# Folding the carried state into the first column of u*B on ScalarE, for ten of sixteen states

## The reference, cut to what matters

```
dt = softplus(einsum(dt_raw, W_dt) + b_dt)
A  = -exp(A_log)
dA  = exp(dt[..., None] * A)
dBx = dt[..., None] * Bm[:, :, None, :] * x[..., None]
def step(h, inp):
    dA_t, dBx_t, C_t = inp
    h = dA_t * h + dBx_t
    y = einsum('bds,bs->bd', h, C_t)
    return (h, y)
x = layernorm(x + scan + Dp * x)
x = layernorm(x + ffn(x))
```

## Time and profile before

| | |
|---|---|
| median of 3 runs | 2003.35 us (2001.41 to 2003.37) |
| profiled execution: time, span | 1997.66 us, 1995.8 us |
| PE busy | 1763.8 us (88%) |
| DVE busy | 1823.0 us (91%) |
| ACT busy | 1568.9 us (79%) |
| POOL busy | 1701.3 us (85%) |

### The profile page before, as it was taken

The page is one execution under the profiler, slowest core; times in us unless marked ns, Lnnn a source line. Parts: engine busy times, 40 slices in busy tenths (PEclk is TensorE's granted clock), DMA queues, the critical chain, the costliest instruction groups (busy, mean ns, idle before and its releaser), DMA issues.

```text
span 1995.8 us, 37091 instructions
## 1 busy us (share of the span) xinstructions
PE 1763.8 (88%) x11048; PEld 1384.4 (69%) x11048; DVE 1823.0 (91%) x2285; ACT 1568.9 (79%) x2924; POOL 1701.3 (85%) x779
## 2 busy tenths in 40 slices
PE   5788888988989988889888989889889898899986
PEld 4667677776777776777666777667767667776764
DVE  4899999999999999999999999999999999999994
ACT  6878878788887788778788787888777887887862
POOL 5998888898888988888888888988889888889880
PEclk7999999999999999999999999999999999999999
DMA  7323333333233233234233233232333332342300
GB/s 243 101 97 120 105 114 117 102 110 117 90 122 124 93 116 116 91 118 133 80 121 117 96 117 126 87 122 97 116 118 98 114 116 87 118 133 70 122 12 22
DMA packets 116565, 215.35 MB, mean 108 GB/s; under 512 B 11153, under 2 KB 45554, under 8 KB 116466
## 3 DMA queue, kind: packets, MB, share of 16 engines
q1 hardware_dynamic: 116466, 214.40, 32.8%
HBM read 195.48 MB, written 18.87 MB: 107 GB/s over the span
## 4 chain that ended last, share of the span: by engine, by line
PE 56%; issue 17%; DVE 16%; ACT 6%; POOL 3%; DVEq 1%; ACTq 0%; DMA 0%; POOLq 0%; SPq 0%
PE p_o L1001 17%; PE p_y L964 12%; DVE h L703 8%; PE p_m L988 6%; PE p_da L932 6%; PE p_c L941 3%; PE p_m L904 3%; DVE hid L747 3%; PE p_m L912 3%; PE p_y L957 2%; PE p_m L978 2%; DVE silu_g L741 2%; ACT da_k L537 2%; ACT p_da L537 1%; POOL ub L410 1%
## 5 line engine op out<-in xcount | busy, mean ns | idle before, releaser
L420 POOL TENSOR_TENSOR h<-h,c_bc 128x1024 f32<-128x1024 f32 x352 | 833.0, 2371 | 148.0 <-ACT h_carry L523 120.7
L410 POOL TENSOR_TENSOR ub<-u,b_bc 128x1024 f32<-128x1024 f32 x320 | 757.7, 2374 | 0.1
L964 PE MATMUL p_y<-ident,h 128*128 128x128 f32 x4096 | 533.3, 277 | 7.7 <-POOL h L420 4.4
L537 ACT ACTIVATE p_da<-dt,neg_a 128x512 f32<-128x512 f32 x640 | 432.1, 682 | 85.3 <-DVE h L703 81.8
L964 PEld LDWEIGHTS p_y<-ident,h 128*128 128x128 f32 x4096 | 476.2, 143 | 28.1 <-POOL h L420 13.6
L703 DVE TENSOR_TENSOR_SCAN h<-p_da,ub 128x512 f32<-128x512 f32 x320 | 381.1, 1213 | 29.8 <-ACT p_da L537 23.6
L703 DVE TENSOR_TENSOR_SCAN h<-p_da,h_carry,ub 128x512 f32<-128x512 f32 x320 | 399.9, 1271 | 1.4 <-ACT p_da L537 0.8
L551 ACT ACTIVATE ub_t<-u_t,bc_t 128x256 f32<-128x256 f32 x768 | 344.9, 497 | 28.9 <-issue 28.1
L1001 PE MATMUL p_o<-wt_down,hid 128*128 128x256 f32 x1536 | 354.8, 382 | 11.8 <-DVE hid L747 8.6
L932 PE MATMUL p_da<-ident,ub_t 128*128 128x128 f32 x1536 | 244.1, 296 | 126.5 <-DVE h L703 125.5
L1001 PEld LDWEIGHTS p_o<-wt_down,hid 128*128 128x128 f32 x1536 | 284.9, 190 | 67.3 <-issue 29.6
(11 more groups left out here) (101 smaller groups left out, 1813.4 us busy)
## 6 DMA issues: line engine op xcount, KB each, us to landing
c_bc<-bc_rows_dram SPq DMA_DIRECT2D x352, 256.0 KB, 5.1
b_bc<-bc_rows_dram SPq DMA_DIRECT2D x128, 512.0 KB, 5.3
x_in<-in_L_attn_x SPq DMA_DIRECT2D x32, 512.0 KB, 3.5
b_bc<-bc_rows_dram SPq DMA_DIRECT2D x64, 256.0 KB, 3.1
out_x<-res_n SPq DMA_DIRECT2D x32, 512.0 KB, 3.3
bc_rows_dram<-bc_rows SPq DMA_DIRECT2D x32, 64.0 KB, 1.6
hid<-in_L_ffn_w_gate SPq DMA_DIRECT2D x1, 768.0 KB, 4.9
hid<-in_L_ffn_w_up SPq DMA_DIRECT2D x1, 768.0 KB, 6.7
```

The source lines that it names most:

```text
L410: nc.gpsimd.tensor_tensor(ub[:, i % UB_SLOTS, :, :], u[:, par, :, :], b_bc[:, i:i + 1, :].broadcast_to([P, DH, T]), ALU.mult).then_inc(s_u ...
L420: nc.gpsimd.tensor_tensor(h[:, s % H_SLOTS, :, :], h[:, s % H_SLOTS, :, :], c_bc[:, i:i + 1, :].broadcast_to([P, DH, T]), ALU.mult).then_i ...
L537: nc.scalar.activation(da, dt[:, par, q, :], ACT.Exp, scale=neg_a[:, q, s:s + 1]).then_inc(s_da, 1)
L964: ins = nc.tensor.matmul(p_y_tok[:, k, q * P:(q + 1) * P], h[:, s % H_SLOTS, q, k * P:(k + 1) * P], ident[:, :], start=False, stop=(s == S ...
```

## The change

In par 1, for the ten B_STATES, DVE's scan no longer takes its initial value from `h_carry`: it takes the constant 0.0. To make that right, ACT first adds decay(first step) times carried state to the first column of u*B in `ub`, for each state and each q (`first_column`, 20 instructions of 128x1 in a par 1 chunk, in place), one state ahead and directly ahead of the decay of the same state and q. The decays of the first step for all states are made in par 0 by two instructions of 128x16 (`first_decay`, at state 8, zone 0). The scans of par 1 wait for the new semaphore s_first, for each q, and no longer for s_ub and s_carry. The six K_STATES stay as they are.

```
+    "first_decay": (8, 0), ...
+FIRST_AHEAD = 1
...
+            def first_decay(c, par, batch):
+                act.wait_ge(s_dt, c + 1)
+                for q in range(DH):
+                    nc.scalar.activation(da_first[:, q, :], neg_a[:, q, :], ACT.Exp,
+                                         scale=dt[:, par, q, 0:1]).then_inc(s_da_first, 1)
+
+            def first_column(c, s, batch, q):
+                i = B_STATES.index(s)
+                if q == 0:
+                    act.wait_ge(s_ub, NB * c + (i + 1))
+                    act.wait_ge(s_da_first, DH * (batch + 1))
+                    act.wait_ge(s_carry, units(batch, s))
+                column = ub[:, i % UB_SLOTS, q, 0:1]
+                nc.scalar.activation(column, da_first[:, q, s:s + 1], ACT.Identity, bias=column,
+                                     scale=h_carry[:, s, q:q + 1]).then_inc(s_first, 1)
...
+                        if nxt and par == 0 and due("first_decay"):
+                            first_decay(c + 1, 1, batch)
+                        cf, sf, pf = unit_at(c, s, FIRST_AHEAD, par)
+                        if core and pf == 1 and (sf >= FIRST_AHEAD or nxt) and sf in B_STATES:
+                            first_column(cf, sf, batch, zone)
                         if core and (se >= DA_AHEAD or nxt):
                             decay(ce, se, pe_, zone)
...
-                    if q == 0:
+                    if par == 1:
+                        dve.wait_ge(s_first, DH * (NB * batch + i) + q + 1)
+                    elif q == 0:
                         dve.wait_ge(s_ub, NB * c + (i + 1))
...
-                if par == 0:
+                if par == 0 or s in B_STATES:
                     initial = 0.0
```

More of the change, by code:

```diff
@@ L39 @@
     "u_transposed0": (8, 2), "u_out0": (14, 0), "u_transposed1": (15, 1), "u_out1": (15, 0),
[1 row of a table removed]
+    "first_decay": (8, 0), "z_out": (2, 0), "stats1": (3, 2), "mean1": (4, 0), "norm_inputs": (6, 1), "scalars": (6, 1), "norm1": (7, 1),
     "x1_transposed": (8, 0), "x1_high": (8, 0), "x1_low": (9, 0),
@@ L131, in mamba_ffn_block @@
         h_carry = sb("h_carry", [P, N, DH], F32)
+        da_first = sb("da_first", [P, DH, N], F32)
         z = sb("z", [P, TT, D], F32)
@@ L208, in mamba_ffn_block @@
         s_carry = sem("s_carry")
+        s_da_first = sem("s_da_first")
+        s_first = sem("s_first")
         s_c_ps = sem("s_c_ps")
```

## The result

The changed kernel takes 2011.36 us (median of 9 runs, 2006.84 to 2015.75), the kernel before 2002.57 us (9 runs): a ratio of 1.005, 95% interval 1.0038 to 1.0061, slower by 8 to 12 us. The forecast was slower, 2022.5 us, with a range from 2004 to 2036: the direction and the mechanism were right, the size was twice too large.

A forecast was written before the change was run, and what follows sets the result against it. PE was taken to bound a par 1 chunk until state 5's scan, DVE after it, with ACT just ahead. Delays of 15.2 us (par 1) and 4.2 (par 0) made 19.4 on 2003.35: 2022.8 us, range 2004 to 2036.

The forecast's parts named there:

- PE bounds the first part, DVE the second, and ACT runs just ahead of DVE: Par 1 chunk, split at state 5's scan: PE busy 21.28 of 21.28 us, then DVE 39.16 of 39.65, ACT 32.00.
- The price of a fold: On ACT, priced from norm L563: busy 0.38 us, holding ACT 0.28; bounds 0.09 (copy of a carry) and 0.38 (no overlap).
- Where it lands: Par 1 delays at states 6, 7, 9 and 13, chunk ending 0.95 us late; par 0 state 9, 0.28 late.
- I take 0.20 as the smallest lead: Least time from a decay's end on ACT to its DVE scan, from one observed hand-over of 0.21 us.
- The sum: 16 par 1 chunks at 0.95 and 15 par 0 chunks at 0.28: 19.4 us more, giving 2022.8 us.
- What DVE saves: Par 1 scans 0.06 us shorter each; 12 of 20 count, 0.70 us a chunk, 11.1 us in all.
- The wait for PE at state 5: Expected profile sign: DVE's wait for `p_da` from PE there, 2.08 us before, about 0.2 us longer.
- DVE's busy time: Expected profile sign: DVE's busy time down by some 18 us while the span grows.
- A cheap fold: Rival: a fold holds ACT only 0.09 us, like the copy of a carry; 1997.5 us; 8 in 100.
- slack leads: Rival: ACT could start decays earlier, so 11.1 to 18.6 us come back, about 1988 us; 4 in 100.
- a costlier fold: Rival: a fold holds ACT 0.38 us without overlap, plus its three waits; 33.3 us more, 2036.7 us; 14 in 100.
- POOL is far ahead: Against the rival that folds wait for POOL's `ub`: DVE waited for it once in the run; no own share.

The follow-up runs named there:

- e3: Kernel before plus folds and first decays on ACT written to a spare tile nobody reads, scans still starting from h_carry; 2020.47 us, ratio 1.0105.
- e10: Kernel before with par 1 initial value 0.0 for the ten B states, their carried state left out, DVE's s_carry wait kept; 1984.38 us, ratio 0.9923.
- e6: The change with folds for states 6, 7 and 9 only, the other seven B states starting from h_carry; 2016.87 us, ratio 1.0073 to the kernel before.
- e7: The change with folds for states 0, 1, 3, 4, 11, 13 and 14 only; 1997.86 us, ratio 0.9978 to the kernel before.
- e1: Kernel before plus only the two 128x16 first-step decays on ACT in par 0, no folds; 2001.31 us, ratio 1.0007.
- e12: Kernel before with DVE's wait for the decay written last in the scan for the ten B states only; 1996.27 us, ratio 0.9972.
- e2: Kernel before with par 1 initial value 0.0 for the ten B states, carried state left out, scans having dropped a wait; 1994.76 us, ratio 0.9971.
- e4: Changed kernel with DVE's wait for the decay written last, directly ahead of the scan; 2010.63 us, ratio 1.006 to the kernel before.
- e5: Kernel before with DVE's wait for the decay written last in the scan; 2000.47 us, ratio 0.9994.
- e8: The change with folds made on POOL, ACT making only the first decays, at state 12 instead of 8; 2007.75 us, ratio 1.0027 to the kernel before.

## Why the prediction was right

- *PE bounds the first part, DVE the second, and ACT runs just ahead of DVE.* Shown: the first part stays at 21.27 or 21.28 us in the changed kernel, in e3 and in e10, whatever DVE and ACT do in it.
- *The price of a fold.* 0.38 us busy and 0.28 us of ACT's time were predicted from L563; measured 375 ns and 0.28. The copy as a lower bound and 0.38 as an upper one were not needed.
- *Where it lands.* In the second part DVE waits longest at state 7 and 9, q=1 (0.38 and 0.28 us, against 0.14 at most elsewhere), and e6 and e7 show it apart from the trace: the six folds of states 6, 7 and 9 cost 15 us, fourteen elsewhere nothing.
- *The step that was mis-sized* is "I take 0.20 as the smallest lead". It came from a scan of q=0, and I used it for q=1 too. Measured: 0.21 for q=0, 0.12 for q=1 in par 1 of the changed kernel, 0.03 for q=1 in par 0. With those, state 7 is 0.86 - 0.08 = 0.78 us late (measured, mean of 14 chunks, from state 5's scan: 7.43 to 8.16, 0.73), state 9 (0.78 - 0.06) + 0.56 - 0.37 + 0.12 = 1.03 (measured 15.97 to 17.05, 1.09), and par 0 0.40 - 0.32 + 0.03 = 0.11 instead of 0.28 (measured 0.10 at the scan, 0.08 at the end of the chunk). The par 1 chunk ends 0.86 us late instead of 0.95. Par 0 is the larger miss: 15 chunks at 0.28 were 4.2 us, and are 1.3.
- *The sum.* 0.86 and 0.08 in fifteen chunks each make 14.1 us, less 0.27 in the last chunk, which was counted at 0.95 late and is shorter than before. The timed runs say 8 to 12. The difference of 2 to 6 us is not settled, so only the direction and the place of the cost are shown, and not its size to the microsecond. Single executions of one kernel spread by 9 us here, and each profile is one of them. That the chunks of the kernel before ran fast in its profile is not it: e1 and e12, which have no folds, have par 1 chunks of 60.85 and 60.91 us against its 60.90. A part of the spread lies outside the chunks: in the traces the first scan starts at 26 or at 28 us, and behind the last scan there are 48.2 or 49.9 us in most, whatever the kernel.
- *What DVE saves* was also too small, 11 us where e10 shows 15: from the second scan of state 8 to the first of state 9, across x1_low, e10 takes 3.74 us in the mean where the kernel before takes 3.87, and the last chunk gives all of its twenty scans. In the changed kernel this has little weight, because ACT sets the time at states 6, 7 and 9.
- *Two signs did not come.* The wait for PE at state 5 was to grow by 0.2 us and fell from 2.08 to 2.00: the folds of state 4 don't disappear in ACT's wait, DVE waits 0.43 us at that state, and this takes up most of what its shorter scans save there. It costs nothing, since PE bounds that part. And DVE's busy time fell by 9.6 us (1823.0 to 1813.4), not by 18, because of the overlap told above.
- *The rivals.* A cheap fold and slack leads are out by the trace; a costlier fold too. That POOL is far ahead was right: no scan waited for `ub` in the loop.

## What to carry to other kernels

An engine at 79% can have no room at all in the 17 us that matter: measure the lead of each of its results over their use before giving it more work, and put new work where it waits for another engine. Of a trade of 90 us on one engine for 18 us on another, neither number decides; the places do where the lead is smaller than the work put ahead of them (1.12 us of folds ahead of state 7's second scan, against a lead of 0.27). Before believing that an edit of one engine's program brought nothing, look at the packets of the instruction queue: with six instructions fewer in the loop, DVE's program came with 64 packets more here (e2 against e10), and 10 us went with them.

## What the runs showed of the hardware that I had not expected

*The hand-over to a scan hangs on where the wait is written.* In the kernel before and in the changed one, DVE's scan starts 0.21 us after the decay when two instructions of the queue (register operations and waits that stand on their own) run between the decay's end and the scan (q=0: at 1083.79 and 1083.90 in the changed kernel, ahead of the scan at 1083.96), 0.12 when there is one (at 1085.48, scan at 1085.56), and 0.03 when the scan itself carries it. With the wait moved onto the scan, 0.21 became 0.03 at every place of q=0 in the loop where DVE waits for ACT (e4, e5). Behind the loop the same line of code gave the opposite: at state 4 of the last par 0 chunk the lead is 0.03 us in the kernel before and 0.13 in e5, so where a wait is written does not by itself decide which instruction carries it. The Trainium skill ("Perfetto Trace Analysis", Sequencer-only Instruction and DVE / Act Engine Instruction) has an instruction wait for its semaphores in a wait queue while the sequencer goes on, whereas an instruction of the sequencer waits in it and is followed by the fetch of the next: that fits the three numbers, some 0.09 us for each instruction between.

*Programs of DVE that differ by a handful of waits behave differently at the loop's edge.* 82 to 84 packets on the instruction queue in most kernels, 146 and 147 in e2 and e8. In the trace of those two, the first instruction of DVE's queue behind the branch of the loop comes 2.7 to 3.1 us after it, in all others 0.3 us. That DVE's instructions are fetched again there is the likely reading, and no run shows it directly. ACT's takes 2.4 to 3.2 us in every kernel here, and shows as a row of the waits of the changed kernel:

```profile
ACT ub_t L571 <- issue: 28.3, 13, 2.3
```

What decides it is open. Counted in the traces, DVE runs 329 instructions in a pass of the loop in e2 and in e8, and 334 to 357 in all the others, so the length of the program is not excluded; nor is the place at which the loop begins, which no run varies alone.
